# Four of the eight value heads' output products made of rounded parts in a fused cross-attention kernel

## The chip, the cores and the metric

The kernel runs on one core of one Trainium2 chip. The metric is the device time of one execution in microseconds (us). Three runs of the kernel before gave 356.71, 356.77 and 357.55 us; the median is 356.77 us.

The engines are named as in the profile. PE is TensorE's matmul queue and PEld its weight loads, DVE is VectorE, ACT is ScalarE, POOL is GpSimd. SP is SyncE, whose queue issues most of the DMAs. Every engine runs its own instructions strictly in the order in which they are written and waits on semaphores.

## The reference

Cross-attention of 2 x 2048 queries of width 512 with 2 x 77 keys of width 384, with 8 heads of width 512, then a residual and a layer norm. Cut to what matters:

```python
Q = (img_embed @ Wq).reshape(B, -1, H, D).transpose(0, 2, 1, 3)
K = (sent_embed @ Wk).reshape(B, -1, H, D).transpose(0, 2, 1, 3)
V = (sent_embed @ Wv).reshape(B, -1, H, D).transpose(0, 2, 1, 3)
score = jnp.einsum('bhqd,bhkd->bhqk', Q, K) / math.sqrt(D)
attn = jax.nn.softmax(jnp.where(mask, score, -jnp.inf), axis=-1)
ctx = jnp.einsum('bhqk,bhkd->bqhd', attn, V).reshape(B, -1, H * D)
out = ctx @ Wo + img_embed
return (out - mu) * jax.lax.rsqrt(var + EPS) * gamma + beta
```

## The kernel before

The keys are few (77 per batch, 154 in all), so the weights are multiplied into the keys and values first. For each head a matrix a = Wq K^T is made (128x4x2x77 per head), and a matrix vw = V Wo. After that a tile of 128 queries needs only x·a for all heads at once (616 columns), a softmax and prob·vw.

**The two stages.** The first stage, some 124 us long, makes a and vw. It has 16 "uses": uses 0 to 7 are the heads' key half (Wk, then Wq), uses 8 to 15 the value half (Wv, then Wo; use u is value head u-8). The second stage walks over 32 query tiles in 16 pairs. It computes the scores in fp32 accuracy from rounded parts with a seven-product scheme, whose right-hand sums T1 to T4 are made on DVE during uses 8 to 11.

**One use.** "Projection u" is ctx times w_proj of use u (4 blocks m of 128 rows; m 0 and 1 are half 0, in the PSUM pair `ps_proj[0]`, m 2 and 3 half 1). "Output product u" multiplies w_out of use u with what the projection gave. PE's order is projection u+1, then output product u, and so on; the projection runs one use ahead. In iteration u ACT drains projection u+1 (`round_kv`), then half 0 and half 1 of output product u (`take_out_product`).

**Two ways to multiply.** `full_product` takes fp32 operands as they are: per block 4 matmuls of 154 columns, each shown as two records in the trace, so 32 records per output product. `short_product` works with parts: a tensor is rounded to fp32r ("hi", on ACT) and the rest of it is kept as a second fp32r tensor ("lo", on DVE or POOL). Per block it makes 4 matmuls of 308 columns, w_hi times [kv_hi, kv_lo], and 4 of 154, w_lo times kv_hi: also 32 per output product. The results stand in two column ranges of the PSUM bank, `first(pair)` and `second(pair)`, and have to be added. Before the change uses 1 to 7 have the short output product, use 0 and uses 8 to 15 the full one.

**What the short way needs besides PE.** For use u: `round_w_out(u)` on ACT (two halves of 128x1024), `split_w_out(u)` on DVE (the same halves, each after ACT's), `split_kv(u)` on DVE (two of 128x308, each after ACT's `round_kv`), and an addition of the second column range on DVE.

**What PE waits for.** Projection u+1 writes the PSUM pairs that hold projection u, so it waits until that has been drained (`wait_kv`, L460). Output product u waits for its operands and until output product u-1 has been drained from the same pairs (`wait_out`, L496). In uses 10, 12, 13 and 15 `transpose_vw` (L536) puts finished columns of vw through PE after block 2 of the output product; ACT and DVE drain that from `ps_proj[1]` (`split_vw`, L737 and L964), and block 2 of the next projection on PE waits for that drain (L477: `dve_vw_lo`).

**The T sums.** They share DVE's queue. After use 8's DVE work stand the ten steps of T1 and T2 (`right_sum`, L982, in place L995), after use 9's the splits of T1 (L1000) and four steps of T4, after use 10's the splits of T2 and six steps of T3, after use 11's the splits of T4 and T3. ACT rounds each T (`round_t`, L779) in iterations 9, 10 and 11, ahead of that iteration's `take_out_product`. The x tiles of the second stage load once all T parts are split and w_out of use 15 has been issued (SP, L367 and L399).

Of the kernel before, what the change touches and what calls it, by code (L numbers as in the profile page):

```python
# [26 lines left out]
F32 = mybir.dt.float32  # L27
F32R = mybir.dt.float32r
I32 = mybir.dt.int32
ALU = mybir.AluOpType  # L30
# [3 lines left out]
P = 128  # L34
# [45 lines left out]
def build(nc, x_tiles, x_rows, ctx_t, wk, wq_t, wv, wo, mask, gamma, beta, out):  # L80
    s = Shapes(x_tiles, ctx_t, wk, wo, mask)
    T, H, USES = s.tiles, s.heads, 2 * s.heads
# [4 lines left out]
    FULL_PROJ, FULL_OUT = 3, 1  # L87
# [13 lines left out]
    with ExitStack() as stack:  # L101
# [3 lines left out]
        def sem(name):  # L105
            return stack.enter_context(nc.semaphore(name))
# [37 lines left out]
        w_proj_lo = [sb(f"w_proj_lo{n}", [P, s.dim_t, s.ctx_t, P], F32R) for n in range(W_RING)]  # L144
        w_out_lo = [sb(f"w_out_lo{n}", [P, s.model_t, s.dim_t, P], F32R) for n in range(W_RING)]
        with ExitStack() as values:
            v_t = [values.enter_context(nc.sbuf_tensor(f"v_t{n}", [P, s.dim_t, s.toks], F32)) for n in range(2)]
        kv_t = [sb(f"kv_t{n}", [P, s.dim_t, 2 * s.toks], F32R) for n in range(2)]
        with ExitStack() as spare:
            t_tmp3 = spare.enter_context(nc.sbuf_tensor("t_tmp3", [P, KT, s.half], F32))  # L150
# [39 lines left out]
        kv_full = prob1[:, :].rearrange("p (m k) -> p m k", m=s.dim_t)  # L190
# [19 lines left out]
        ps_outp = pairs[2:4]  # L210
# [22 lines left out]
        act_ctx_hi, act_p_hi, act_o_hi = sem("act_ctx_hi"), sem("act_p_hi"), sem("act_o_hi")  # L233
        act_kv_hi, act_a_hi, act_vw_t, act_vw_hi = sem("act_kv_hi"), sem("act_a_hi"), sem("act_vw_t"), sem("act_vw_hi")
# [7 lines left out]
        dve_kv_lo, dve_rest = sem("dve_kv_lo"), sem("dve_rest")  # L242
# [2 lines left out]
        dve_pt_lo, dve_resid, dve_stats, dve_mv = sem("dve_pt_lo"), sem("dve_resid"), sem("dve_stats"), sem("dve_mv")  # L245
        dve_ve, dve_rows, dve_t, dve_t_lo = sem("dve_ve"), sem("dve_rows"), sem("dve_t"), sem("dve_t_lo")
        dve_comb, dve_half_max = sem("dve_comb"), sem("dve_half_max")
        dve_centred, dve_zero, dve_pad, dve_last = sem("dve_centred"), sem("dve_zero"), sem("dve_pad"), sem("dve_last")

        pool_const, pool_p_lo = sem("pool_const"), sem("pool_p_lo")  # L250
# [20 lines left out]
        def second(pair):  # L271

            return pair[:, :, s.toks:2 * s.toks]

        def by_batch(ap):
            return ap.rearrange("p m (b k) -> p m b k", b=s.batches)

        def head_cols(t, half, h):

            return t[:, 2 * half:2 * half + 2, :, h * s.keys:(h + 1) * s.keys]  # L280
# [25 lines left out]

        def whole_out(u):

            return u < FULL_OUT or u >= H

        def value_of(u):

            return kv_full if u < FULL_OUT else v_t[u % 2][:, :, :]

        def use_w_out(u):

# [126 lines left out]
        def _(pe):  # L443
# [16 lines left out]
            def wait_kv(u, half):  # L460

                if whole_out(u):
                    pe.wait_ge(act_kv_hi, 2 * u + half + 1)
                else:
                    pe.wait_ge(dve_kv_lo, 2 * (u - FULL_OUT) + half + 1)

            def project_full(u):

# [27 lines left out]
            def wait_out(u, half):  # L496

                if u < H:
                    pe.wait_ge(dve_a_lo, 2 * u + half + 1)
                else:  # L500
                    pe.wait_ge(act_vw_t, 2 * (u - H) + half + 1)

            def out_product_full(u):

# [17 lines left out]
            def out_product(u):  # L522

                wait_kv(u, 1)
                for m in range(s.model_t):
                    half = m // 2
                    if m % 2 == 0:
                        pe.wait_ge(act_o_hi, 2 * (u - FULL_OUT) + half + 1)
                        pe.wait_ge(dve_o_lo, 2 * (u - FULL_OUT) + half + 1)
                        wait_out(u - 1, half)  # L530
                    mm = short_product(ps_outp[half], m % 2, w_out_hi[u % 2], w_out_lo[u % W_RING],
                                       kv_t[u % 2], m, s.dim_t)
                    if m % 2:
                        mm.then_inc(pe_outp, 1)

            def transpose_vw(h):  # L536
                for j, b in plan[h]:
                    n, rows = group_no[j, b], s.key_rows(j)
                    pe.wait_ge(act_vw_t, 2 * h)
                    if n >= 2:  # L540
                        pe.wait_ge(dve_vw_lo, n - 1)
                    if h < H - 1:
                        wait_kv(H + h + 1, 1)
                    elif h == H - 1:
                        wait_kv(USES - 1, 0)
                    for m in range(s.model_t):
                        mm = pe.transpose(ps_vw(h, b)[0:rows, m * P:(m + 1) * P],
                                          vw_t[:, m, b, j * P:j * P + rows], identity[:, :])
                    mm.then_inc(pe_vw, 1)
# [146 lines left out]
        def _(act):  # L696
# [141 lines left out]
            for u in range(USES):  # L838
                if u + 1 < USES:
                    round_kv(u + 1)  # L840
                if u + 2 < USES and not whole(u + 2):
                    round_w_proj(u + 2)
                if u == H + 1:
                    for part in T_PARTS[:4]:
                        round_t(*part)
                elif u in (H + 2, H + 3):
                    for part in T_PARTS[2 * (u - H):2 * (u - H) + 2]:
                        round_t(*part)
                if u == USES - 2:
                    round_blocks(0)  # L850
                    round_sums(0)
                elif u == USES - 1:
                    round_blocks(1)
                take_out_product(u, 0)
                if u == USES - 1:
                    seed(0)
                if u >= H:
                    split_vw(u - H)
                if u + 1 < H:
                    round_w_out(u + 1)  # L860
                take_out_product(u, 1)
            copy_s1(0)
# [37 lines left out]
        def _(dve):  # L900
# [14 lines left out]
            def split_w_out(u):  # L915

                for half in range(2):
                    dve.wait_ge(act_o_hi, 2 * (u - FULL_OUT) + half + 1)
                    dve.tensor_tensor(half_cols(w_out_lo[u % W_RING], half), half_cols(w_out_sb[u % W_RING], half),
                                      half_cols(w_out_hi[u % 2], half).bitcast(F32), ALU.subtract)\  # L920
                       .then_inc(dve_o_lo, 1)
# [26 lines left out]
            def take_out_product(u, half):  # L948

                pair = ps_outp[half]  # L950
                if u < FULL_OUT:
                    dve.wait_ge(act_a_hi, 2 * u + half + 1)
                    dve.tensor_tensor(head_cols(a_lo, half, u), by_batch(first(pair)),
                                      head_cols(a_hi, half, u).bitcast(F32), ALU.subtract).then_inc(dve_a_lo, 1)
                else:
                    r = by_batch(next_rest()[:, :, :])
                    dve.wait_ge(act_a_hi, 2 * u + half + 1)
                    dve.tensor_tensor(r, by_batch(first(pair)), head_cols(a_hi, half, u).bitcast(F32), ALU.subtract)\
                       .then_inc(dve_rest, 1)
                    dve.wait_ge(dve_rest, rests[0])  # L960
                    dve.tensor_tensor(head_cols(a_lo, half, u), by_batch(second(pair)), r, ALU.add)\
                       .then_inc(dve_a_lo, 1)

            def split_vw(h):  # L964
                for j, b in plan[h]:
                    rows = s.key_rows(j)
                    dve.wait_ge(act_vw_hi, group_no[j, b] + 1)
                    if rows < P:
                        dve.wait_ge(dve_pad, 2 * s.batches)
                    dve.tensor_tensor(vw_lo[0:rows, b, j, :], ps_vw(h, b)[0:rows, 0:s.model],  # L970
                                      vw_hi[0:rows, b, j, :].bitcast(F32), ALU.subtract).then_inc(dve_vw_lo, 1)
# [157 lines left out]
            split_ctx()  # L1129
            bias_of_mask()  # L1130
            for u in range(USES):
                if u + 1 < H:
                    split_kv(u + 1)
                if u < H:
                    take_out_product(u, 0)
                    if u + 1 < H:
                        split_w_out(u + 1)
                    take_out_product(u, 1)
                else:
                    if u == USES - 1:  # L1140
                        bias_rows()
                    split_vw(u - H)
                if u == H:
                    for n in (T1, T2):
                        for b in range(s.batches):
                            right_sum(n, b)
                elif u in (H + 1, H + 2):
                    for n in ((T1, T4), (T2, T3))[u - H - 1]:
                        for b in range(s.batches):
                            split_t(n, b) if n in (T1, T2) else right_sum(n, b)  # L1150
                elif u == H + 3:
                    for n in (T4, T3):
                        for b in range(s.batches):
                            split_t(n, b)
# [204 lines left out]
```

## Time and profile before

| | us |
|---|---|
| median of 3 runs | 356.77 |
| the profiled execution | 356.75 |
| its span, first to last instruction | 355.0 |
| PE busy | 348.2 (98%) |
| DVE busy | 269.3 (76%) |
| ACT busy | 231.2 (65%) |
| POOL busy | 192.9 (54%) |

The profiled execution's time is 1.75 us above its span. PE is busy nearly all the time; the matmul records overlap, so the time that a series of matmuls takes is read from the start of one group to the start of the next and not from the duration of one record.

### The profile page before, as it was taken

How to read it: one execution, taken by the hardware profiler on the slowest of the kernel's cores; microseconds unless marked ns; L12 is line 12 of the kernel's file. 1: busy time of each engine (PE TensorE's matmuls, PEld its weight loads, DVE VectorE, ACT ScalarE, POOL GpSimd, SP SyncE). 2: the span in 40 equal slices, each digit the busy share in tenths (PEclk: the TensorE clock that was granted, in tenths of full speed). 3: DMA queues.
4: the chain of work that ended last, by engine and by line, in shares of the span. 5: the costliest groups of instructions: out<-in, count | busy, mean ns of one | idle time of the engine just before them, and what ended most of it. 6: DMA issues, size and time to landing. Idle time of an engine off the chain costs nothing. (4 is left out here: it accounts for less than half of the span.)

```text
span 355.0 us, 6790 instructions
## 1 busy us (share of the span) xinstructions
PE 348.2 (98%) x2271; PEld 323.6 (91%) x2271; DVE 269.3 (76%) x501; ACT 231.2 (65%) x780; POOL 192.9 (54%) x208
## 2 busy tenths in 40 slices
PE   8999999999999999999999999999999999999994
PEld 6999999999999999988899889889988998899883
DVE  3299998673911267898798888987987989789895
ACT  3377764244333669877786876877778868768560
POOL 0045640000003858679769688688696796885243
PEclk9999999999999999999999999999999999999998
DMA  7998679766644080043141341440532413413012
GB/s 262 409 423 318 254 238 348 266 245 210 225 152 187 0 292 6 3 178 116 64 176 54 126 151 50 160 144 35 179 100 80 162 65 130 149 41 110 31 49 100
DMA packets 19682, 55.80 MB, mean 157 GB/s; under 512 B 1728, under 2 KB 3264, under 8 KB 17728
## 3 DMA queue, kind: packets, MB, share of 16 engines
q1 hardware_dynamic: 18784, 54.38, 42.7%
q10 hardware_dynamic: 864, 1.00, 0.9%
q8 instruction: 18, 0.29, 0.3%
q14 instruction: 16, 0.13, 0.1%
HBM read 46.98 MB, written 8.39 MB: 156 GB/s over the span
## 5 line engine op out<-in xcount | busy, mean ns | idle before, releaser
L628 PE MATMUL pair<-vw_hi,pt_hi 128*128 128x512 f32 x155 | 62.2, 401 | 0.0
L628 PE MATMUL pair<-vw_hi,pt_lo 128*128 128x512 f32 x155 | 61.0, 393 | 0.0
L628 PE MATMUL pair<-vw_lo,pt_hi 128*128 128x512 f32 x155 | 60.7, 392 | 0.0
L1230 POOL TENSOR_TENSOR out_sb<-centred,beta_sb 128x512 f32<-128x512 f32 x30 | 38.8, 1293 | 26.8 <-ACT centred L820 26.7
L1250 POOL TENSOR_TENSOR x_sum<-xt_in 128x256 f32<-128x256 f32 x16 | 11.9, 745 | 62.2 <-DMA xt_in<-x_tiles 62.0
L775 ACT ACTIVATE prob<-c,neg_max 128x77 f32<-128x77 f32 x128 | 43.9, 346 | 0.0
L1275 POOL TENSOR_TENSOR xo_lo<-x_sum,xo_hi 128x512 fp32r<-128x512 f32 x32 | 41.2, 1293 | 0.5 <-ACT xo_hi L799 0.5
L557 PE MATMUL pair<-a_hi,xo_hi 128*128 128x308 f32 x128 | 40.4, 316 | 0.0
L813 ACT ACTIVATE pt_hi<-pair 128x640 fp32r<-128x640 f32 x32 | 22.5, 702 | 26.9 <-PE pair L615 26.9
L557 PE MATMUL pair<-a_lo,xo_hi 128*128 128x308 f32 x128 | 38.9, 304 | 0.0
L1076 DVE TENSOR_TENSOR pair<-pair,x_in 128x512 f32<-128x512 f32 x31 | 21.7, 700 | 22.6 <-PE pair L628 22.4
L557 PE MATMUL pair<-a_hi,xo_lo 128*128 128x308 f32 x128 | 38.8, 303 | 0.0
L456 PE MATMUL pair<-ctx_sb,w_proj 128*128 128x154 f32 x264 | 36.3, 294 | 0.0
L456 PEld LDWEIGHTS pair<-ctx_sb,w_proj 128*128 128x128 f32 x264 | 35.2, 189 | 0.8 <-DMA ctx_sb<-ctx_t 0.8
L1281 POOL TENSOR_TENSOR w_proj_lo<-w_proj,w_proj_hi 128x768 fp32r<-128x768 f32 x10 | 18.4, 1869 | 32.0 <-ACT w_proj_hi L711 32.0
L1269 POOL TENSOR_TENSOR xo_lo<-xt_in,xo_hi 128x512 fp32r<-128x512 f32 (+1 forms) x32 | 33.1, 1035 | 4.6 <-ACT xo_hi L792 3.2
L456 PE MATMUL pair<-v_t,w_out 128*128 128x154 f32 x256 | 35.5, 294 | 0.0
L628 PEld LDWEIGHTS pair<-vw_hi,pt_lo 128*128 128x128 f32 x155 | 29.1, 188 | 6.6
L456 PEld LDWEIGHTS pair<-v_t,w_out 128*128 128x128 f32 x256 | 34.2, 189 | 0.0
L628 PEld LDWEIGHTS pair<-vw_lo,pt_hi 128*128 128x128 f32 x155 | 29.2, 188 | 5.3
L628 PEld LDWEIGHTS pair<-vw_hi,pt_hi 128*128 128x128 f32 x155 | 29.1, 188 | 5.1
L1224 POOL TENSOR_TENSOR rstd<-var_eps,minus_half 128x1 f32<-128x1 f32 x32 | 17.6, 550 | 29.5 <-DVE var_eps L1097 29.5
(117 smaller groups left out, 958.7 us busy)
## 6 DMA issues: line engine op xcount, KB each, us to landing
w_out<-wo SPq DMA_DIRECT2D x8, 1024.0 KB, 4.8
xt_in<-x_tiles SPq DMA_DIRECT2D x16, 512.0 KB, 4.1
x_in<-x_rows SPq DMA_DIRECT2D x16, 512.0 KB, 4.8
out<-out_sb SPq DMA_DIRECT2D x31, 256.0 KB, 2.2
w_out<-wq_t SPq DMA_DIRECT2D x7, 1024.0 KB, 6.9
w_proj<-wv SPq DMA_DIRECT2D x8, 768.0 KB, 4.6
w_proj<-wk SPq DMA_DIRECT2D x6, 768.0 KB, 9.2
w_out<-wq_t SPq DMA_DIRECT2D x2, 512.0 KB, 7.6
```

Source lines behind the costliest of these rows:

```text
L456: mm = pe.matmul(pair[:, bank, 0:s.toks], w[:, m, k, :], moving[:, k, 0:s.toks], start=(k == 0), stop=(k == tiles - 1))
L557: mm = pe.matmul(bank[:, 0:s.half], xs[:, left, k, :], r[:, k, :], start=(begin and k == 0 and n == 0), stop=(k == KT - 1 and n == len(pas ...
L628: mm = pe.matmul(ps_out[:, i % 2, 0:s.model], ps[:, j, :], v[:, b, j, :], start=(j == 0 and n == 0), stop=(j == s.key_t - 1 and n == len(p ...
L775: e = act.activation(prob[i % 2][:, cols], c2[:, cols], ACT.Exp, bias=neg_max[i % 2][:, h:h + 1], accum_out=sums[i % 2][:, h:h + 1])
L813: act.activation(pt_hi[i % 2][:, :, :], pt_blocks, ACT.Copy).then_inc(act_pt_hi, 1)
L1076: dve.tensor_tensor(y, ps_out[:, i % 2, 0:s.model], x_in[c % X_RING][:, i % CHUNK, :], ALU.add)\
L1224: pool.tensor_tensor(rstd[i % 2][:, :], var_eps[i % 2][:, :], minus_half[:, :], ALU.pow).then_inc(pool_rstd, 1)
L1230: pool.tensor_tensor(out_sb[i % OUT_RING][:, :], centred[i % 2][:, :], beta_sb[:, :], ALU.add)\
L1250: pool.tensor_tensor(sum1, a21, a22, ALU.add).then_inc(pool_sum, 1)
L1269: pool.tensor_tensor(xo_lo[p % 2][:, blocks, :, :], src, xo_hi[p % 2][:, blocks, :, :].bitcast(F32), ALU.subtract).then_inc(pool_xo_lo, 1)
L1275: pool.tensor_tensor(xo_lo[p % 2][:, blocks, :, :], x_sum[:, at:at + 2, :, :], xo_hi[p % 2][:, blocks, :, :].bitcast(F32), ALU.subtract).t ...
L1281: pool.tensor_tensor(half_cols(w_proj_lo[u % W_RING], half), half_cols(w_proj_sb[u % W_RING], half), half_cols(w_proj_hi[u % 2], half).bit ...
```

## The change

Uses 8, 10, 12 and 14 (value heads 0, 2, 4, 6) get the short output product. `whole_out` now names only use 0 and the odd uses of the value half as full. Where the semaphore counts were u - FULL_OUT, they are now counted by `split_before(u)`, the number of short uses ahead of u; `summed_before(u)` counts the additions on DVE in the value half.

In the value half ACT copies the first column range to vw_t as before, and DVE then adds the second range in place (`add_out_product`, new semaphore `dve_vw_sum`). PE's `wait_out` after an even value use waits for that addition, and `wait_kv` of an even use waits for DVE's split instead of ACT's copy. The transposes of vw wait for the additions too. The values of odd value heads move to a buffer that lies over kv_t1, since kv_t0 now holds the parts of the even heads; w_out_hi0 alone is used for the rounded weights.

```diff
-            return u < FULL_OUT or u >= H
+            return u < FULL_OUT or (u >= H and u % 2 == 1)
...
-            return kv_full if u < FULL_OUT else v_t[u % 2][:, :, :]
+            return kv_full if u < FULL_OUT else v_t[:, :, :]
...
-                    pe.wait_ge(dve_kv_lo, 2 * (u - FULL_OUT) + half + 1)
+                    pe.wait_ge(dve_kv_lo, 2 * split_before(u) + half + 1)
...
+                elif whole_out(u):
+                    pe.wait_ge(act_vw_t, 2 * (u - H) + half + 1)
                 else:
-                    pe.wait_ge(act_vw_t, 2 * (u - H) + half + 1)
+                    pe.wait_ge(dve_vw_sum, summed_before(u) + half + 1)
...
+                    if m == 2 and u >= H:
+                        transpose_vw(u - H)
...
                     pe.wait_ge(act_vw_t, 2 * h)
+                    pe.wait_ge(dve_vw_sum, summed_before(H + h))
...
-                if u + 1 < H:
+                if u + 1 < USES and not whole_out(u + 1):
                     round_w_out(u + 1)
                 take_out_product(u, 1)
...
+            def add_out_product(u, half):
+
+                cols = head_cols(vw_t, half, u - H)
+                dve.wait_ge(act_vw_t, 2 * (u - H) + half + 1)
+                dve.tensor_tensor(cols, by_batch(second(ps_outp[half])), cols, ALU.add).then_inc(dve_vw_sum, 1)
...
             for u in range(USES):
-                if u + 1 < H:
+                if u + 1 < USES and not whole_out(u + 1):
                     split_kv(u + 1)
                 if u < H:
                     take_out_product(u, 0)
-                    if u + 1 < H:
+                    if not whole_out(u + 1):
                         split_w_out(u + 1)
                     take_out_product(u, 1)
                 else:
+                    if not whole_out(u):
+                        add_out_product(u, 0)
                     if u == USES - 1:
                         bias_rows()
                     split_vw(u - H)
+                    if u + 1 < USES and not whole_out(u + 1):
+                        split_w_out(u + 1)
+                    if not whole_out(u):
+                        add_out_product(u, 1)
                 if u == H:
                     for n in (T1, T2):
                         for b in range(s.batches):
                             right_sum(n, b)
```

**Place 1, DVE ahead of the T sums.** Before, the first step of T1 (prob1<-a_hi) follows directly on use 7's last drain (a_lo<-pair3):

```order
L961 TENSOR_TENSOR a_lo<-pair2,rest1 128x4x77
L958 TENSOR_TENSOR rest0<-pair3,a_hi 128x308
L961 TENSOR_TENSOR a_lo<-pair3,rest0 128x4x77
L995 TENSOR_TENSOR prob1<-a_hi 128x616
L995 TENSOR_TENSOR t_tmp4_0<-prob1,a_lo 128x616
```

Now, in the changed program, the weights of use 8 are split there (w_out_lo2) and both halves of output product 8 are added (vw_t<-pair2, vw_t<-pair3):

```order
L976 TENSOR_TENSOR a_lo<-pair2,rest1 128x4x77
L934 TENSOR_TENSOR w_out_lo2<-w_out2,w_out_hi0 128x1024 x2
L973 TENSOR_TENSOR rest0<-pair3,a_hi 128x308
L976 TENSOR_TENSOR a_lo<-pair3,rest0 128x4x77
L983 TENSOR_TENSOR vw_t<-pair2,vw_t 128x4x77
L983 TENSOR_TENSOR vw_t<-pair3,vw_t 128x4x77
L1016 TENSOR_TENSOR prob1<-a_hi 128x616
L1016 TENSOR_TENSOR t_tmp4_0<-prob1,a_lo 128x616
```

The ten T steps moved behind the drain of output product 8.

**Place 2, DVE from the end of T2 to the first transposes' drain.** Before (t_tmp3 is the last step of T2, t_lo the splits of T1, then four steps of T4, then vw_lo, the drain of the transposes in use 10):

```order
L995 TENSOR_TENSOR t_tmp4_1<-a_hi,xt_in1 128x616
L995 TENSOR_TENSOR t_tmp3<-t_tmp4_1,a_lo 128x616
L1000 TENSOR_TENSOR t_lo0<-xt_in0,t_hi0 128x616
L1000 TENSOR_TENSOR t_lo1<-xt_in1,t_hi1 128x616
L995 TENSOR_TENSOR t_tmp4_0<-a_hi,prob1 128x616
L995 TENSOR_TENSOR xt_in0<-t_tmp4_0,a_lo 128x616
L995 TENSOR_TENSOR t_tmp4_1<-a_hi,t_tmp3 128x616
L995 TENSOR_TENSOR xt_in1<-t_tmp4_1,a_lo 128x616
L970 TENSOR_TENSOR vw_lo<-pair1,vw_hi 128x512 x2
```

Now (kv_t0 is the split of projection 10, w_out_lo1 that of use 10's weights, vw_t<-pair2 the addition for half 0 of output product 10):

```order
L1016 TENSOR_TENSOR t_tmp3<-t_tmp4_1,a_lo 128x616
L950 SCALAR_TENSOR_TENSOR kv_t0<-pair0,kv_t0 128x2x154
L950 SCALAR_TENSOR_TENSOR kv_t0<-pair1,kv_t0 128x2x154
L934 TENSOR_TENSOR w_out_lo1<-w_out1,w_out_hi0 128x1024 x2
L1021 TENSOR_TENSOR t_lo0<-xt_in0,t_hi0 128x616
L1021 TENSOR_TENSOR t_lo1<-xt_in1,t_hi1 128x616
L1016 TENSOR_TENSOR t_tmp4_0<-a_hi,prob1 128x616
L1016 TENSOR_TENSOR xt_in0<-t_tmp4_0,a_lo 128x616
L1016 TENSOR_TENSOR t_tmp4_1<-a_hi,t_tmp3 128x616
L1016 TENSOR_TENSOR xt_in1<-t_tmp4_1,a_lo 128x616
L983 TENSOR_TENSOR vw_t<-pair2,vw_t 128x4x77
L991 TENSOR_TENSOR vw_lo<-pair1,vw_hi 128x512 x2
```

Four instructions on which PE or ACT depend now stand between T sums, and the drain of the transposes has the addition ahead of it. The same pattern stands once more in uses 11 and 12, after the six steps of T3.

**Place 3, ACT in iteration 9.** Before (t_hi are the rounded T1 and T2, vw_t<-pair2 and pair3 the drains of output product 9, v_t1 those of projection 11):

```order
L781 ACTIVATE t_hi0<-prob1 128x616
L781 ACTIVATE t_hi1<-t_tmp3 128x616
L735 ACTIVATE vw_t<-pair2 128x4x77
L735 ACTIVATE vw_t<-pair3 128x4x77
L728 ACTIVATE v_t1<-pair0 128x308
```

Now:

```order
L796 ACTIVATE t_hi0<-prob1 128x616
L796 ACTIVATE t_hi1<-t_tmp3 128x616
L750 ACTIVATE vw_t<-pair2 128x4x77
L734 ACTIVATE w_out_hi0<-w_out1 128x1024 x2
L750 ACTIVATE vw_t<-pair3 128x4x77
L743 ACTIVATE v_t<-pair0 128x308
```

The rounding of use 10's weights stands behind the rounding of T1 and T2, which waits for DVE's T steps, and ahead of the drain of half 1.

## Rows read from the trace of the kernel before

**Rows 1.** Who made PE wait: us in total, times, longest (the other: Rows 9).

```profile
PE pair L449 <- DVE w_out_lo L919: 0.3, 1, 0.3
```

**Rows 2.** PE in order of time, value half: start, us, line, operation, records.

```profile
68.26 4.36 PE L456 MATMUL pair<-v_t,w_out 128*128 128x154 f32 x32
72.46 3.31 PE L456 MATMUL pair<-ctx_sb,w_proj 128*128 128x154 f32 x24
...
79.81 3.31 PE L456 MATMUL pair<-ctx_sb,w_proj 128*128 128x154 f32 x24
82.96 3.31 PE L456 MATMUL pair<-v_t,w_out 128*128 128x154 f32 x24
...
88.03 3.31 PE L456 MATMUL pair<-ctx_sb,w_proj 128*128 128x154 f32 x24
...
103.60 3.31 PE L456 MATMUL pair<-ctx_sb,w_proj 128*128 128x154 f32 x24
...
124.28 0.41 PE L557 MATMUL pair<-a_hi,xo_hi 128*128 128x308 f32 x1
```

**Rows 3.** PE in order of time, key half: output product 5's first record, projection 7's.

```profile
46.82 0.30 PE L449 MATMUL pair<-kv_t,w_out_hi 128*128 128x308 f32 x1
...
50.85 0.30 PE L449 MATMUL pair<-ctx_split,w_proj_hi 128*128 128x308 f32 x1
```

**Rows 4.** DVE in order of time, value half.

```profile
66.80 0.80 DVE L995 TENSOR_TENSOR prob<-a_hi 128x616 f32<-128x616 f32 x1
...
74.39 0.80 DVE L995 TENSOR_TENSOR t_tmp<-t_tmp,a_lo 128x616 f32<-128x616 f32 x1
76.87 1.51 DVE L1000 TENSOR_TENSOR t_lo<-xt_in,t_hi 128x616 fp32r<-128x616 f32 x2 [1.68 <-ACT t_hi L781]
...
80.89 0.80 DVE L995 TENSOR_TENSOR xt_in<-t_tmp,a_lo 128x616 f32<-128x616 f32 x1
87.37 1.29 DVE L970 TENSOR_TENSOR vw_lo<-pair,vw_hi 128x512 fp32r<-128x512 f32 x2 [5.68 <-ACT vw_hi L743]
88.58 0.79 DVE L1000 TENSOR_TENSOR t_lo<-prob,t_hi 128x616 fp32r<-128x616 f32 x1
...
93.43 1.64 DVE L995 TENSOR_TENSOR t_tmp<-t_tmp,a_lo 128x616 f32<-128x616 f32 x2
...
96.40 1.51 DVE L1000 TENSOR_TENSOR a_lo<-t_tmp,a_hi 128x616 fp32r<-128x616 f32 x2
```

**Rows 5.** ACT in order of time, key half (w_out_hi) and value half.

```profile
56.42 2.00 ACT L719 ACTIVATE w_out_hi<-w_out 128x1024 fp32r<-128x1024 f32 x2
...
72.66 0.43 ACT L735 ACTIVATE vw_t<-pair 128x308 f32<-128x308 f32 x1 [1.67 <-PE pair L456]
...
77.95 0.71 ACT L781 ACTIVATE t_hi<-t_tmp 128x616 fp32r<-128x616 f32 x1
...
86.74 1.09 ACT L743 ACTIVATE vw_hi<-pair 128x512 fp32r<-128x512 f32 x2 [1.06 <-PE pair L547]
```

**Rows 6.** Line L919: ns of one, minimum, median and maximum, first and last start.

```profile
L919 DVE TENSOR_TENSOR w_out_lo<-w_out,w_out_hi x14: 1208/1218/2575, 17.0 to 58.8; 128x1024 fp32r<-128x1024 f32 x14
```

**Rows 7.** Group of DVE line L935: busy us, mean ns, idle before.

```profile
L935 DVE SCALAR_TENSOR_TENSOR kv_t<-pair,kv_t 128x308 fp32r<-128x308 f32 x4 | 1.8, 474 | 1.3 <-ACT kv_t L728 1.3
```

**Rows 8.** The two w_out_lo before output product 1 on DVE.

```profile
17.00 2.36 DVE L919 TENSOR_TENSOR w_out_lo<-w_out,w_out_hi 128x1024 fp32r<-128x1024 f32 x2 [3.08 <-ACT w_out_hi L719]
```

**Rows 9.** PE in order of time: the start of the program, and output product 1.

```profile
1.19 3.16 PE L651 MATMUL pair<-zeros 128*128 128x512 bf16 x7 [1.19 <-DVE zeros L901]
4.31 6.53 PE L456 MATMUL pair<-ctx_sb,w_proj 128*128 128x154 f32 x48
...
18.48 0.38 PE L449 MATMUL pair<-kv_t,w_out_hi 128*128 128x308 f32 x1 [0.30 <-DVE w_out_lo L919]
```

**Rows 10.** PE in order of time: the last matmul of the program.

```profile
349.54 0.28 PE L645 MATMUL pair<-vw_hi,pt_lo 128*128 128x256 f32 x1
```

**Rows 11.** Stretch: its us, busy us of PE, PEld, DVE, ACT, POOL, PEclk, DMA, GB/s.

```profile
352.00:352.50 0.50, 0.00 (x0) 0.00 (x0) 0.22 (x1) 0.00 (x0) 0.00 (x0) 0.87 0.07 16
```

More of the change, by code:

```diff
@@ L146, in build @@
         with ExitStack() as values:
-            v_t = [values.enter_context(nc.sbuf_tensor(f"v_t{n}", [P, s.dim_t, s.toks], F32)) for n in range(2)]
+            values.enter_context(nc.sbuf_tensor("gap6", [P, s.dim_t, 2 * s.toks], F32))
+            v_t = values.enter_context(nc.sbuf_tensor("v_t", [P, s.dim_t, s.toks], F32))
         kv_t = [sb(f"kv_t{n}", [P, s.dim_t, 2 * s.toks], F32R) for n in range(2)]
@@ L247, in build @@
         dve_comb, dve_half_max = sem("dve_comb"), sem("dve_half_max")
+        dve_vw_sum = sem("dve_vw_sum")
         dve_centred, dve_zero, dve_pad, dve_last = sem("dve_centred"), sem("dve_zero"), sem("dve_pad"), sem("dve_last")
@@ L307, in whole_out, with split_before, summed_before @@
         def whole_out(u):
-            return u < FULL_OUT or u >= H
+            return u < FULL_OUT or (u >= H and u % 2 == 1)
+        def split_before(u):
+            return sum(not whole_out(v) for v in range(u))
+        def summed_before(u):
+            return 2 * sum(not whole_out(v) for v in range(H, u))
         def value_of(u):
-            return kv_full if u < FULL_OUT else v_t[u % 2][:, :, :]
+            return kv_full if u < FULL_OUT else v_t[:, :, :]
         def use_w_out(u):
@@ L527, in out_product @@
                     if m % 2 == 0:
-                        pe.wait_ge(act_o_hi, 2 * (u - FULL_OUT) + half + 1)
-                        pe.wait_ge(dve_o_lo, 2 * (u - FULL_OUT) + half + 1)
+                        pe.wait_ge(act_o_hi, 2 * split_before(u) + half + 1)
+                        pe.wait_ge(dve_o_lo, 2 * split_before(u) + half + 1)
                         wait_out(u - 1, half)
@@ L917, in split_w_out @@
                 for half in range(2):
-                    dve.wait_ge(act_o_hi, 2 * (u - FULL_OUT) + half + 1)
+                    dve.wait_ge(act_o_hi, 2 * split_before(u) + half + 1)
                     dve.tensor_tensor(half_cols(w_out_lo[u % W_RING], half), half_cols(w_out_sb[u % W_RING], half),
```

## The prediction

> **What bounds the kernel now.** I read first who made PE wait: it lost 0.3 us to another engine once [rows 1] and 1.2 us before its first matmul [rows 9]. So the time is PE's own work, and every wait added to PE adds to the time unless PE gets it back. Then PE in order of time, for what one product takes. A full output product starts at 68.26 and the next projection at 72.46: 4.20 us. A full projection runs from 79.81 to 82.96: 3.15 us. Output product 10, which has transposes behind block 2, runs from 82.96 to 88.03: 5.07 us, 0.87 more [rows 2]. The short output product of the key half starts at 46.82 and is followed at 50.85: 4.03 us [rows 3]. Both kinds have 32 records: 131 ns apart in the full one, 126 ns in the short. Last I read DVE and ACT in order of time across the value half, because they have the new work, and both are strict queues [rows 4, 5].
>
> **What PE gains.** 4.20 - 4.03 = 0.17 us per output product, four times: 0.68 us. That is all: the short product has as many matmuls as the full one has records, and the fewer columns hardly show. By the Trainium skill (TensorE: Matmul & The Clock Gate, "Back-to-back issue gap") a lone matmul of N columns takes about N/2.4 + 2.5 ns; by that a 308- and a 154-column matmul would take 198 ns together, 3.2 us per product, and the gain would be some 4 us over four. The row of this kernel says 252 ns per pair, so I go by the row. (By the rule only products 12 and 14 would help, since what PE gains ahead of the last stall found below only lengthens the stalls: 2 x 0.8 us, some 360.7 us in the end; inside my range, and the row speaks against it.)
>
> **What DVE and ACT get, per even value use.** ACT: the rounding of the weights, 2.00 us for both halves [rows 5]. DVE: the split of the weights, 2.36 us for two when POOL is idle [rows 8], 1.2 each at the least and at the median, 2.6 at the most [rows 6]; two splits of the projection at 0.47 [rows 7]; two additions, which no row shows. The nearest row is that same split, which reads the same PSUM columns: 0.47, taken as 0.48. Over four uses that is 8 us on ACT and 17 us on DVE. Neither engine is full there, so what counts is where this stands in the queues.
>
> **The wait for the T sums.** Times are on the clock of the profile of before; "now" is my reckoning.
>
> Step 1, the T sums start late. Before, T1's first step ran at 66.80 and T2's last at 74.39, ending 75.19: 8.39 us for ten steps, one dependent on the other [rows 4]. Now they stand behind the additions of output product 8. That product starts at 68.26 as before (product 7 starts at 68.26 - 3.15 - 4.03 = 61.1 and its half 0 is drained by 63.8; ACT then rounds for 2.0 us and DVE, 1.2 us behind, has the weights split by about 67.1) and ends at 72.29. ACT began its drain 0.20 us after the product's end (72.66 against 72.46) and took 0.43 [rows 2, 5], so half 1 is drained at 72.92 and added at 73.44. T1 starts at 73.4 and T2 ends at 81.8, 6.6 us later than before.
>
> Step 2, first stall. Projection 11 on PE now waits for DVE's split of projection 10, which stands right behind T2: 81.7 to 82.2. For the way from DVE's end to PE's start I take 0.25 us: the first of the two w_out_lo ended at 17.00 + 1.2 = 18.2 and PE started at 18.48 [rows 8, 9]. So projection 11 starts at 82.45. PE is free at 72.29 + 3.15 + 4.20 = 79.64. **Stall 2.8 us.**
>
> Step 3, the next products. ACT rounds T2's last part until 82.5 (0.71 each [rows 5]), drains output product 9, half 0, by 82.8, rounds the weights of use 10 from 82.7 to 84.7. DVE splits them by 85.05 and 86.2. Projection 11 ends at 85.60 and output product 10 can start then, with 0.3 us in hand after 0.25 for the way; with w_out_lo at 1.8 us, a little above the median, it would start 0.3 late. It would end at 85.60 + 4.03 + 0.87 = 90.50.
>
> Step 4, second stall. DVE goes on with the two splits of T1 and four steps of T4. Before they took 76.87 to 81.69, 4.82 us [rows 4]; now 86.15 to 91.0. ACT rounds T4's second part until 91.7, and only then drains half 0 of output product 10 (to 92.0); DVE adds it by 92.5, while ACT drains the transposes. Before, ACT began on these at 86.74 and DVE had finished at 88.66, 1.92 us later [rows 4, 5]; now 92.0 and 93.95. Projection 12's block 2 waits for that: without a wait PE is there at 90.50 + 1.57 = 92.07, with it at 94.2. **Stall 2.1 us.** Projection 12 ends at 95.77.
>
> Step 5, third stall. DVE adds half 1 (to 94.3), splits T2 and makes T3: before 88.58 to 95.07, 6.49 us [rows 4]; now 94.25 to 100.75. Then comes the split of projection 12, done at 101.1, for which projection 13 waits: start 101.35. PE is free at 95.77 + 4.20 = 99.97. **Stall 1.4 us.**
>
> Step 6, the rest. Output product 12 starts at 104.5 and ends at 109.4; it began its successor at 103.60 before [rows 2]. ACT rounds its weights from 101.7 and DVE has the first half at 104.0: 0.2 us in hand. The splits of T4 and T3 (before 94.98 to 97.91 [rows 4]) end at 108.0, before output product 12 ends, so the x tiles, whose load is queued behind the weight load that waits for this product, go out no later against PE than before. In uses 13 to 15 no T sums are left; the additions and the last weight split stand between works that end well ahead of PE. I cost them at nothing. What hides them is the 3.15 us projection ahead of each output product; if w_out_lo took 2.6 us a half there, beside POOL's work, output product 14 would wait about 1 us.
>
> **Sum.** 2.8 + 2.1 + 1.4 = 6.3 us of stalls, less 0.7 gained: +5.6 us, so the second stage starts at 124.28 + 5.6 = 129.9. That stage is PE's own work again. The profiled execution took 356.75 us (span 355.0), against a median of 356.77. Forecast **362.3 us**. The three stalls are one chain: DVE's from 73.4 to 101.1 hardly depends on PE. So what makes PE late in the middle is taken back from the next stall, and the end is set by the last link. With no time on the way from DVE to PE it is 362.0; with slow weight splits (1.8 a half) DVE's chain gets 1.2 longer in step 3, and product 12 waits another 0.3 for its own: 363.8.
>
> **The clock.** PE's granted clock was 1.00 up to the end, and after the last matmul, at about 349.8, it fell to its lower level, 1.2 GHz for 2.4, within the stretch from 352.0 to 352.5: 0.87 is its mean there [rows 10, 11]. So about 2.6 us after PE fell still the clock went down, and the first stall is 2.8 us. What a fall costs: the program's first seven matmuls take 3.12 us to the next group, and from there 48 matmuls go at 133 ns, the full rate [rows 9]. Half of 3.1 us is 1.6 us at most. But a loss after the first stall is swallowed by the second, and most of one after the second by the third; only one after the third would stay. The skill's page (section "Why this matters for your kernels") warns of idle gaps between bursts of matmuls for this reason; by that rule the time would be up to 363.9, the rival below.
>
> **The rivals.**
> 1. The chain holds and the clock falls after the third stall, or the weight splits run slow: 363.5 to 365. For it: rows 10 and 11, and the 2.6 us at most in rows 6. Against: the third stall is the shortest, and POOL is idle. 0.17.
> 2. Only the first stall, since DVE's steps pack closer than I reckon or PE's lateness frees the others: 356.75 + 2.8 - 0.7 = 358.9, up to 360. Against: the T steps' times are rows, and ACT's and DVE's orders are fixed. 0.12.
> 3. It ends on the other side: the T sums don't delay PE, because DVE reaches the split of projection 10 by 79.4. It would decide from a T chain that starts 2.8 us earlier, at 70.6, that is if it stood behind the addition of half 0 alone. Then only the 0.68 us are left: 356.1, not slower than before. For it: PE's own work does get shorter [rows 3], and DVE has idle time in total. Against: the order (place 1) has both additions ahead of T1. 0.05, and 0.04 for a mixture, 355.7 to 357.9, that cannot be told from no change.
> 4. Something past the third stall is late as well, say the x tiles or POOL's parts of the first tiles: above 365. 0.04.
>
> That leaves 0.58 for the forecast's own neighbourhood, 361 to 363.5. I give the range 359.5 to 365.0. A measurement of this kernel can tell about 0.3% (1.1 us) from no change. Faster by over that (under 355.7) only if rival 3 gains beyond its 0.7, or part of a cost elsewhere goes: 0.03; within it 0.06; slower 0.91.
>
> **What would show it.** In the changed profile PE's list of waits has three new entries behind DVE: kv_t (L950), some 2.8 and 1.4 us, and vw_lo (L991), some 2.1 us; projection 11 starts near 82.45, block 2 of projection 12 near 94.2, projection 13 near 101.35, the second stage near 129.9. The first T step stands near 73.4. A short output product takes 4.03 us. It is wrong if PE's wait for DVE after use 8 is under 1 us, if the four short products take less than 3.9 us, if PE's clock shows less than 1.00 between 80 and 110, or if the second stage itself gets longer.

## The result, and the profile after

The changed kernel takes 362.11 us (median of 4 runs, 361.87 to 362.60) against 357.16 us before (4 runs, 356.71 to 357.56). The ratio is 1.0141, with a 95% interval of 1.0129 to 1.0153: 5.0 us slower. The forecast was 362.3. The profiled execution took 362.15 us, with a span of 360.4, so the two profiled executions differ by 5.4 us.

One stretch carries the comparison below: from the start of projection 9 on PE to the first matmul of the second stage. It leaves out the start of the program, where single profiles differ by some tenths of a microsecond. Before it lasts 59.16 us (65.12 to 124.28, the end in [rows 2]), after it 64.59 (65.46 to 130.05): **5.43 us longer**. The forecast had 5.6. The start of the stretch in both profiles, before and after:

```profile
65.12 3.31 PE L456 MATMUL pair<-ctx_sb,w_proj 128*128 128x154 f32 x24
```

```profile
65.46 3.31 PE L466 MATMUL pair<-ctx_sb,w_proj 128*128 128x154 f32 x24
```

So the changed kernel's profile is 0.34 us late at this point. "On the clock of before", further down, means with these 0.34 us taken off.

First, who made PE wait in the changed kernel (us in total, times, longest), answering [rows 1]:

```profile
PE pair L466 <- DVE kv_t L950: 3.6, 2, 2.5
PE pair L666 <- DVE zeros L916: 1.2, 1, 1.2
PE pair L466 <- DMA w_proj<-wk: 0.4, 1, 0.4
```

Before, DVE's L919 had held PE up for 0.3 us in all. Now two waits for the split of a projection make 3.6. The wait for vw_lo that step 4 announced is not in the list.

PE in order of time, value half of the changed kernel (start, us, line, operation, records), answering [rows 2]:

```profile
72.65 3.31 PE L466 MATMUL pair<-ctx_sb,w_proj 128*128 128x154 f32 x24
75.80 4.36 PE L466 MATMUL pair<-v_t,w_out 128*128 128x154 f32 x32
82.62 5.06 PE L466 MATMUL pair<-ctx_sb,w_proj 128*128 128x154 f32 x24 [2.46 <-DVE kv_t L950]
87.41 0.42 PE L459 MATMUL pair<-kv_t,w_out_hi 128*128 128x308 f32 x1
...
92.43 3.62 PE L466 MATMUL pair<-ctx_sb,w_proj 128*128 128x154 f32 x24
95.89 4.36 PE L466 MATMUL pair<-v_t,w_out 128*128 128x154 f32 x32
101.42 3.39 PE L466 MATMUL pair<-ctx_sb,w_proj 128*128 128x154 f32 x24 [1.17 <-DVE kv_t L950]
104.53 0.41 PE L459 MATMUL pair<-kv_t,w_out_hi 128*128 128x308 f32 x1
...
109.55 3.31 PE L466 MATMUL pair<-ctx_sb,w_proj 128*128 128x154 f32 x24
...
130.05 0.41 PE L572 MATMUL pair<-a_hi,xo_hi 128*128 128x308 f32 x1
```

Output product 9 starts at 75.80 and takes 4.20, so PE is free at 80.00; projection 11 starts at 82.62. That is the first stall, 2.62 us. Projection 11 itself then takes 4.79 us up to 87.41, where 3.15 was usual. Projection 12 takes 3.46, 0.31 too much. Projection 13 starts at 101.42 where PE was free at 95.89 + 4.20 = 100.09: 1.33 us.

Why projection 11 is slow stands in the busy times by stretch of the changed kernel (us of the stretch, then busy us of PE, PEld, DVE, ACT and POOL, then PEclk, DMA share, GB/s):

```profile
80.00:81.00 1.00, 0.16 (x2) 0.00 (x0) 0.97 (x2) 0.55 (x1) 0.00 (x0) 1.00 0.06 25
82.50:83.00 0.50, 0.38 (x3) 0.41 (x4) 0.35 (x1) 0.50 (x2) 0.00 (x0) 1.00 0.93 393
83.00:86.00 3.00, 3.00 (x14) 3.00 (x14) 1.88 (x2) 2.65 (x5) 0.00 (x0) 0.51 0.41 172
86.00:87.00 1.00, 1.00 (x8) 1.00 (x7) 1.00 (x2) 0.13 (x1) 0.00 (x0) 0.76 0.00 0
87.00:88.00 1.00, 1.00 (x11) 1.00 (x9) 1.00 (x3) 0.29 (x1) 0.00 (x0) 1.00 0.00 0
```

The granted clock went to its lower level (1.2 GHz) just after PE had started again, at about 83.05, and came back near 86.5.

DVE in order of time, the same kernel, answering [rows 4]:

```profile
73.31 0.48 DVE L983 TENSOR_TENSOR vw_t<-pair,vw_t 128x308 f32<-128x308 f32 x1 [1.54 <-ACT vw_t L750]
73.71 0.79 DVE L1016 TENSOR_TENSOR prob<-a_hi 128x616 f32<-128x616 f32 x1
...
81.28 0.80 DVE L1016 TENSOR_TENSOR t_tmp<-t_tmp,a_lo 128x616 f32<-128x616 f32 x1
82.00 0.86 DVE L950 SCALAR_TENSOR_TENSOR kv_t<-pair,kv_t 128x308 fp32r<-128x308 f32 x2
84.12 2.36 DVE L934 TENSOR_TENSOR w_out_lo<-w_out,w_out_hi 128x1024 fp32r<-128x1024 f32 x2 [1.27 <-ACT w_out_hi L734]
...
92.80 1.29 DVE L991 TENSOR_TENSOR vw_lo<-pair,vw_hi 128x512 fp32r<-128x512 f32 x2
94.01 0.47 DVE L983 TENSOR_TENSOR vw_t<-pair,vw_t 128x308 f32<-128x308 f32 x1
...
100.80 0.86 DVE L950 SCALAR_TENSOR_TENSOR kv_t<-pair,kv_t 128x308 fp32r<-128x308 f32 x2
```

T1's first step starts as the addition of output product 8's half 1 ends, at 73.71 where it stood at 66.80 before. The two splits (L950) follow T2 and T3 without a gap: DVE is at work all the time that PE waits for it. The drain vw_lo (L991, ending at 94.09) comes by way of ACT: DVE idles 1.10 us before the addition ahead of it, until ACT, which had to round T4 first, has copied half 0 of output product 10.

### The profile page after: what moved, and what is told of

It is laid out like the page before. It is cut to its first block and busy times, and to the rows that moved or that the text cites. A ratio compares the mean times of both kernels' runs of the same rounds, so it can differ in the third digit from the quotient of the medians.

```text
span 360.4 us, 6840 instructions
## 1 busy us (share of the span) xinstructions
PE 349.8 (97%) x2271; PEld 324.9 (90%) x2271; DVE 285.0 (79%) x525; ACT 238.8 (66%) x788; POOL 193.0 (54%) x208
## 5 line engine op out<-in xcount | busy, mean ns | idle before, releaser
L459 PE MATMUL pair<-kv_t,w_out_hi 128*128 128x308 f32 x176 | 46.4, 338 | 0.0
L466 PE MATMUL pair<-ctx_sb,w_proj 128*128 128x154 f32 x264 | 38.8, 304 | 4.1 <-DVE kv_t L950 3.6
L466 PEld LDWEIGHTS pair<-ctx_sb,w_proj 128*128 128x128 f32 x264 | 37.0, 197 | 5.8 <-issue 4.3
L934 DVE TENSOR_TENSOR w_out_lo<-w_out,w_out_hi 128x1024 fp32r<-128x1024 f32 x22 | 31.6, 1475 | 5.9 <-ACT w_out_hi L734 5.8
L459 PE MATMUL pair<-kv_t,w_out_lo 128*128 128x154 f32 x176 | 35.8, 244 | 0.0
```

The lines of the kernel that those rows point to most:

```text
L459: mm = pe.matmul(pair[:, bank, 0:n], w[:, m, k, :], moving[:, k, 0:n], start=(at == 0), stop=(at == len(steps) - 1))
L466: mm = pe.matmul(pair[:, bank, 0:s.toks], w[:, m, k, :], moving[:, k, 0:s.toks], start=(k == 0), stop=(k == tiles - 1))
```

## The experiments

The theory: PE waits because the T sums stand in DVE's queue ahead of the splits and drains that PE needs (the queue theory). Its rivals: the short products themselves cost (each alike, by contention or latency); the T sums are late and that alone costs; the fall of the clock is part of the 5 us. Each ratio is to the kernel before, timed beside it on the same chip; the times of different rows come partly from different chips. "Stretch" is projection 9 to the second stage, 59.16 us before.

| kernel | us | ratio, 95% interval | stretch, against before |
|---|---|---|---|
| changed | 362.11 | 1.0141, 1.0129 to 1.0153 | +5.43 |
| changed, again | 362.66 | 1.0152, 1.0138 to 1.0166 | +5.44 |
| new places | 356.41 | 0.9976, 0.9966 to 0.9986 | -0.65 |
| kernel before, new places | 357.11 | 0.9999, 0.9991 to 1.0008 | 0.00 |
| kernel before, full key half | 358.03 | 1.0023, 1.0014 to 1.0032 | 0.00 |
| T1 first | 358.60 | 1.0042, 1.0027 to 1.0058 | +1.43 |
| use 8 full | 358.86 | 1.0050, 1.0035 to 1.0065 | +1.58 |
| use 12 full | 361.35 | 1.0119, 1.0105 to 1.0133 | +4.18 |
| kernel before, late sums | 356.82 | 0.9995, 0.9985 to 1.0005 | 0.00 |
| filler | 362.70 | 1.0165, 1.0147 to 1.0182 | +5.43 |
| filler, again | 362.44 | 1.0152, 1.0138 to 1.0166 | +5.43 |

### The T sums in new places

```diff
+            ROUND_SLOT = [1, 2, 2, 4, 6, 6, 7, 8]
...
+            SUM_SLOT, SPLIT_SLOT = [0, 0, 1, 3, 4, 4, 5, 6], [1, 2, 2, 5, 7, 7, 7, 8]
...
                 else:
+                    t_work(2 * (u - H))
                     if not whole_out(u):
                         add_out_product(u, 0)
```

The eight parts in their order (T1, T2, T4, T3, each for both batches) get a slot each. Slot 2(u-8) is the place ahead of the drains of use u, slot 2(u-8)+1 the place behind them, on DVE (`t_work`) and on ACT for the rounding. `right_sum`, `split_t` and `round_t` are unchanged.

> The changed kernel with nothing but the places of the T sums, their roundings and their splits moved: T1 and T2 ahead of the additions of use 8 or spread behind them, T4 ahead of the additions in use 10, T3 in uses 10 and 11, so that by reckoning no instruction that PE waits for stands behind a T step when PE wants it. Queue theory: all three stalls go and only PE's gain stays, 4 x 0.17 us, so about 0.7 us under the kernel before (356.4), and PE waits for DVE nowhere in the value half. Rival, the short products themselves cost (in reads, latency or contention of the extra DVE and ACT work): it stays above the kernel before by a good part of the 5 us.

It is faster than both kernels: 356.41 us, 0.24% under the kernel before, 0.14% to 0.34%. The stretch is 0.65 us shorter than before, against 0.68 reckoned. In PE's waits only the start of the program is left:

```profile
PE pair L666 <- DVE zeros L919: 1.2, 1, 1.2
```

And DVE in order of time shows the same instructions in other places:

```profile
72.88 0.80 DVE L1019 TENSOR_TENSOR xt_in<-t_tmp,a_lo 128x616 f32<-128x616 f32 x1
73.60 0.86 DVE L986 TENSOR_TENSOR vw_t<-pair,vw_t 128x308 f32<-128x308 f32 x2
...
76.62 0.85 DVE L953 SCALAR_TENSOR_TENSOR kv_t<-pair,kv_t 128x308 fp32r<-128x308 f32 x2
```

The split of projection 10 (L953) ends by 77.5 where PE wants it at 80.3. All the extra work of the short products is still there, so its mere presence costs nothing that shows: the first rival falls. This run moves the roundings on ACT together with the sums on DVE; no run moves ACT's alone, so how much of the second stall is ACT's order and how much DVE's is not separated.

### The same places in the kernel before

The same edit, on the kernel without short products in the value half.

> The kernel before (no even value head short) with the same new places of the T sums, roundings and splits as the run with new places. Queue theory: PE waits for none of these, so no difference from the kernel before, within 0.3 us. If it is faster or slower, that part has to be taken off what the short products get credit for in the run with new places.

No difference in the stretch and none in the time. So the gain of the run with new places belongs to the short products.

### The key half full

```diff
-    FULL_PROJ, FULL_OUT = 3, 1
+    FULL_PROJ, FULL_OUT = 3, 8
```

Besides, `value_of` gives v_t for uses 1 to 7, and the roundings and splits for them are left out.

> The kernel before with the output products of uses 1 to 7 made full instead of short (their rounding and splits left out): the opposite of the change, seven times, where nothing stalls. If a short output product is worth 0.17 us on PE, it is slower by 7 x 0.17 = 1.2 us (less some 0.3 us of a wait of use 1 that goes): +0.9 to +1.2. By the rule of lone matmuls (0.8 to 1.0 us each) it would be slower by 6 to 7 us. If the short product gains nothing: no difference.

It is slower by 0.14% to 0.32%, 0.5 to 1.1 us, 0.8 in the middle: a little under the 0.9 to 1.2 that was reckoned, and far from the 6 to 7 us of the rule for lone matmuls. The profiles are sharper than the times. From projection 2 to projection 9 PE takes 50.24 us in the kernel before (14.88 to 65.12) and 50.90 here (15.77 to 66.67), 0.66 more; in the kernel before, output product 1 starts 0.45 us late (18.48 [rows 9], where 14.88 + 3.15 = 18.03), and that delay isn't there here. Together 1.11 us for seven products, **0.16 us each**, the same as the 0.65 us for four in the value half.

### T1 ahead of the additions

The slots again, all as in the changed kernel but T1's sums in slot 0, ahead of the additions of output product 8.

> The changed kernel with the six steps of T1 moved ahead of the two additions of use 8 on DVE, all else in place. DVE idles there before the additions, so T2 ends some 4 to 5 us earlier. Queue theory: the first stall (2.6 us) goes, the second comes back to some 0.6 to 1 us since the clock no longer falls and T4 ends earlier, the third stays at 1.2 to 1.4 us: some 1.2 to 1.8 us over the kernel before, 3.3 to 3.8 us under the changed kernel. Rival, the short products themselves cost: unchanged or nearly so, 361 to 362.

PE's waits:

```profile
PE pair L466 <- DVE kv_t L953: 1.2, 1, 1.2
PE pair L466 <- DVE vw_lo L994: 0.5, 1, 0.5
```

The first stall is gone, by moving six instructions past two, and the clock stays at 1.00. The vw_lo wait that the changed kernel's list had lacked is now there, and the last wait stays at 1.2. The time is 1.5 us over the kernel before, as the queue theory had it.

### Use 8 full, use 12 full

```diff
-            return u < FULL_OUT or (u >= H and u % 2 == 1)
+            return u < FULL_OUT or u == H or (u >= H and u % 2 == 1)
```

For use 12 it is `u == H + 4`. The values of the use that is full stand in the memory of kv_t0.

> The changed kernel with use 8 full again (uses 10, 12 and 14 short): three quarters of the change. Queue theory: T1 and T2 start at 66.8 as before, the first stall is gone; T4 and T3 are still behind the weight splits, so stalls of 0.6 and 1.2 us, less 3 x 0.17 gained: 1.3 to 2.0 us over the kernel before. A rival by which each short product costs alike would leave 3/4 of the 5.0 us, 3.8 us over the kernel before.

> The changed kernel with use 12 full again (uses 8, 10 and 14 short). Queue theory: the split of projection 12, for which projection 13 waited 1.2 us behind T3, isn't there, so the third stall goes (1.3 us from start to start) and one gain of 0.17 with it; the first two links stay: 1.1 us under the changed kernel, 3.8 to 4.0 us over the kernel before. If each short product cost alike, it would be 3.8 as well, but with use 8 full the same rule has already given a number to compare; if the clock's fall in the first stall carried through where no third stall swallows what is late, it would be up to 1.6 more.

The two are mirror images: three short products each, and +1.58 against +4.18 us in the stretch. A cost that each product carries alike would give the same for both. Use 8 full lies in the range expected, 1.3 to 2.0 us (1.8 by its ratio). Use 8 costs much because its additions push all T sums back by 6.6 us; use 12 costs its own stall. The run with use 12 full is a little above the 3.8 to 4.0 us that I had written, 4.3 by its ratio; I had taken 5.0 for the changed kernel in place of the stretch's 5.43. Against that it is 1.25 less, and 1.33 of stall less 0.17 of gain had made 1.16. The clock fell here too, in projection 11; the loss ended in the second stall and did not carry through, so the rival in that expectation falls too.

### Late sums in the kernel before

```diff
                 if n == T1:
                     dve.wait_ge(dve_a_lo, 2 * H)
+                    dve.wait_ge(act_vw_t, 2)
```

> The kernel before, where the first T1 step waits in addition until ACT has drained output product 8 (72.9 on its clock, 6 us later than now), nothing else changed. Queue theory: late T sums alone cost nothing, since without the split of projection 10 no wait of PE stands behind them before the transposes: within 0.3 us of the kernel before. Rival, the T sums are themselves on the path (they gate the first x tiles or the transposes' drain directly): slower by 1 us or more.

T1's first step now starts at 73.35, after 6.44 us of waiting on DVE, and the stretch is the same to 0.01 us. T sums that come 6.4 us late hold nobody up by themselves: DVE still idles 1.59 us before vw_lo. It takes both: sums late, and an instruction for PE behind them.

### A filler in the first stall

```diff
+            def fill():
+                for _ in range(FILL):
+                    pe.matmul(pairs[2][:, 0, 2 * s.toks:BANK], zeros[:, 0:P], zeros[:, 0:BANK - 2 * s.toks],
+                              start=True, stop=True).then_inc(pe_fill, 1)
...
             for u in range(USES):
+                if u == H + 2:
+                    fill()
```

> The changed kernel with 20 matmuls of zeros (204 columns each, into unused columns of one bank) in the first stall, where PE would be idle; ACT's drain of output product 9 waits for them, which by reckoning ends before that drain starts. They should keep the granted clock at 1.00, so that projection 11 takes 3.15 us instead of 4.79. Swallow theory: the 1.6 us so saved come back as a longer second stall (vw_lo, some 1.8 us), and the time stays at that of the changed kernel within 0.3 us. Rival, the clock's fall is part of the 5 us: faster by 1.6 us, 360.5.

PE, then DVE's drain vw_lo, in order of time in the filler kernel, and below them the busy times of the stretch in which the clock had fallen in the changed kernel (the 1.00 ahead of the last two numbers is PEclk):

```profile
80.34 1.91 PE L668 MATMUL pair<-zeros 128*128 128x204 bf16 x20
82.96 3.38 PE L468 MATMUL pair<-ctx_sb,w_proj 128*128 128x154 f32 x24 [0.71 <-DVE kv_t L961]
...
91.10 1.74 PE L468 MATMUL pair<-ctx_sb,w_proj 128*128 128x154 f32 x12
94.58 1.81 PE L468 MATMUL pair<-ctx_sb,w_proj 128*128 128x154 f32 x12 [1.75 <-DVE vw_lo L1002]
```

```profile
93.15 1.29 DVE L1002 TENSOR_TENSOR vw_lo<-pair,vw_hi 128x512 fp32r<-128x512 f32 x2
```

```profile
83.00:84.00 1.00, 1.00 (x8) 1.00 (x9) 0.20 (x1) 1.00 (x3) 0.00 (x0) 1.00 1.02 434
```

Projection 11 is fast again (3.12 us to the next group; the clock is 1.00 from 80 to 110), and the time that it saves comes back in the wait for vw_lo, 1.75 us where the changed kernel had none in its list. DVE did not follow PE's gain: vw_lo ends at 94.44 against 94.09, and this profile's projection 9 had begun 0.35 later (65.81). The stretch is 64.59 us, the same to the hundredth as the changed kernel's. Its time stood 0.6 us above the changed kernel's 362.11, more than the 0.3 us that had been allowed, but the two had not been timed side by side, so both were timed once more on one chip:

> The changed kernel once more, beside the filler on the same chip, for a direct comparison: 361.8 to 362.6.

> The filler kernel once more, beside the changed kernel on the same chip. Swallow theory: the same time as the changed kernel within 0.3 us, or up to 0.3 more (in its profile the stalls began 0.3 us later than in the changed kernel's, since the program began later). Rival, the fall of the clock is part of the 5 us: 1.6 us faster than the changed kernel.

They cannot be told apart: 1.0152 both, with the same interval, and 64.60 and 64.59 us for the stretch. The rival that wanted 1.6 us back falls.

## Why the prediction was right, step by step

**The size of the gain.** 0.17 us per product, from two rows: the run with new places gave 0.65 for four, the full key half 1.11 for seven. Right. The rule for lone matmuls, which the prediction cites from the Trainium skill (TensorE: Matmul & The Clock Gate, "Back-to-back issue gap"), gives 198 ns for a pair where these rows have 252, and so, by an estimate from it, about 1.0 us of gain per product where 0.16 was measured. The measurement decides, as the prediction had chosen.

**Step 1, the T sums start late.** Reckoned 73.4, found 73.71, which is 73.37 on the clock of the profile of before. Right.

**Step 2, the first stall.** Reckoned 2.8 us, found 2.62. Right; the way from DVE's end to PE's start was near 0.15 us (first split from 82.00, 0.47 long, PE at 82.62), not 0.25.

**Step 3 and step 4, the second stall.** Product 10 had its weights in time: w_out_lo took 1.2 us a half (2.36 for two). But the course was another than the step said. I had PE idle for 2.1 us before block 2 of projection 12. What happened is that the clock fell for 3.4 us, and projection 11 and the product behind it took 1.76 us longer (92.43 - 82.62 = 9.81 against 3.15 + 5.07 - 0.17 = 8.05), and only 0.31 us of waiting was left. Their sum is 2.07, as reckoned for the wait alone. That the sum agrees is no luck: DVE finished vw_lo at 94.09, 93.75 on the clock of before (reckoned 93.95), and in the filler kernel it did so at the same place although PE had not been slowed. That there was room for all of the fall was a closer thing: it cost 1.67 us (9.81 with it, 8.14 in the filler kernel), a little more than the "1.6 us at most" of the prediction, and the room was 1.9 us (94.58 - 91.10 - 1.57 in the filler kernel). The forecast of three new waits in PE's list was wrong by one for this reason. Of the signs that I had set down for an error, one came true: PE's clock was under 1.00 between 80 and 110. I had taken that for something that would change the time, in the same text in which I had reckoned that the next stall swallows it; the filler shows the second to be right. As a sign it was badly chosen.

**Step 5, the third stall.** Reckoned 1.4, found 1.33. Right.

**Step 6, the rest.** Projection 14 started 5.61 us later than before, counted from projection 9 (109.55 - 65.46 against 103.60 - 65.12); after that PE waits for no one, and product 14 gains its 0.17. Costed at nothing, and nothing it was: the two halves of w_out_lo took 2.52 us together in use 14. (The prediction calls 1.8 us a half "a little above the median"; the median in [rows 6] is 1.22, so that case was a much slower one than it says, and it did not occur.)

**The sum.** 2.62 + 2.07 + 1.33 = 6.02, and some 0.1 us where projection 13 and product 12 took 8.13 instead of 8.05; less 0.68: 5.4 us. The forecast's 5.6 is high because its last link came early: projection 13 started at 101.08 on the clock of before, 0.27 us ahead of the 101.35 reckoned. 0.1 of it is the way from DVE to PE, the rest is DVE's chain, which ran 0.2 us ahead of the reckoning. That the time itself came within 0.2 us of the forecast is partly luck: the forecast added its 5.6 to 356.75, while the kernel before had a median of 357.16 beside the changed one, and the medians differ by 4.95.

**The rivals' prices.** Rival 3, the other side, was priced wrongly. It said that 0.68 us of gain is all that is left once the first stall is gone. With T1 first that stall was gone and the kernel was still 1.5 us slower: the second and the third stall have causes of their own, the T4 and T3 sums ahead of a drain and of a split. To get to the other side it took new places for T1, T2, T4 and T3 on two engines. Rival 2, the first stall alone at 358.9, was not seen: no run had the first stall without the second. Of rival 1, the clock did fall, but after the first stall and not after the third (1.00 from 87 to 130 us). Of rival 4, nothing past the third stall was late: from the second stage's start to the end of the span it is 230.3 us (360.4 - 130.05), against 230.7 before.

## What to carry to other kernels

When a change puts a small instruction that the bottleneck engine needs on a queue with long background work, reckon when that queue reaches it, not how busy the engine is: DVE was 76% busy before and had the room, and T sums in the wrong places cost nine times what the change gained on PE (6.0 against 0.68 us). If several waits hang on one other engine's chain, add up the chain and not the delays: what makes the bottleneck late in the middle (here a fall of the clock) is taken back by the next wait, as long as it is less than that wait (1.67 of 1.9 us here). And try the places of the background work before giving up a change: here the same arithmetic in another order went from 1.4% slower to 0.24% faster.

## What the runs showed of the hardware

The clock was granted at full level throughout the first stall, in which PE did nothing for 2.5 us, and fell to the lower level only after PE had taken up work again. How long after differs from profile to profile: 0.4 us in the first of the changed kernel (82.62 to 83.07), 1.1 in the second, 1.2 in the one with use 12 full. It stayed down for 3.4 us of full work each time, in projection 11 (0.83 in 80 to 90 us each). With use 12 full, PE's start behind the stall and then the stretches (PEclk is third from the end):

```profile
82.87 5.06 PE L466 MATMUL pair<-ctx_sb,w_proj 128*128 128x154 f32 x24 [2.46 <-DVE kv_t L950]
```

```profile
82.00:84.00 2.00, 1.13 (x9) 1.17 (x10) 1.10 (x3) 1.64 (x3) 0.00 (x0) 1.00 0.86 360
84.00:86.00 2.00, 2.00 (x11) 2.00 (x10) 1.63 (x2) 1.92 (x4) 0.00 (x0) 0.52 0.26 107
86.00:88.00 2.00, 2.00 (x12) 2.00 (x11) 2.00 (x3) 0.04 (x1) 0.00 (x0) 0.63 0.00 0
```

Shorter stalls cost no clock in any profile: idle times of 1.2 us in the changed kernel, of 1.75 us in the filler kernel and of 0.5 us with T1 first, nor did the first stall when 1.9 us of it were filled with matmuls of zeros.

An fp32r matmul of 308 columns and one of 154 take 252 ns together, 126 per matmul, in a series in which each has its own weights to load; the fp32 product of 154 columns takes 131 ns per record and two records per matmul. What sets the 126 was not tested.
